# Audio tower in fp32: widened inverse sums, remainder tiles packed two at a time, and expert rows turned by VectorE

## The reference

```python
h = tok(x)                     # 16 sequences of 128 tokens, 256 features; conv of stride 2, mean, layer norm
h = h + attn0(layernorm(h))    # 16 heads of 16, causal window of 64, softmax, output projection
h = h + ffn0(layernorm(h))     # 16 experts, top 2, F = 352, 320 slots an expert, plus a shared FFN of F = 352
h = h + attn1(layernorm(h))    # 16 heads of 16, causal
h = h + ffn1(layernorm(h))     # 64 experts, top 3, H = 1024, 128 slots an expert, gelu, biases

# ffn0, per expert e: xs[320, 256] are the rows sent to e
y = (silu(xs @ w_gate[e]) * (xs @ w_up[e])) @ w_down[e]      # 352 = 128 + 128 + 96; 320 = 128 + 128 + 64
# attention, per head: out = (exp(scores) @ v) / sum(exp(scores))
```

## Time and profile before

| what | value |
|---|---|
| runs | 1119.18, 1120.36, 1120.80 us |
| median | 1120.36 us |
| span of the profiled execution | 1118.0 us |
| busy: PE, PEld, DVE, ACT, POOL | 1073.2, 906.5, 488.1, 525.8, 320.7 us |
| 0 to 38 us | first loads and the first pair, PE filling up |
| 38 to 200 us | first attention, convolution and router beside it |
| 200 to 230 us | shared FFN, last scatters |
| 230.46 to 422.58 us | the 16 experts of the first FFN |
| 422.58 to 606 us | shared FFN's rest and second attention |
| 606 to 642 us | its end, scatters, first rows of the 64 experts |
| 642.28 us to the end | the 64 experts |

### The profile page before, as it was taken

The page is one execution under the profiler, slowest core; times in us unless marked ns, Lnnn a source line. Parts: engine busy times, 40 slices in busy tenths (PEclk is TensorE's granted clock), DMA queues, the critical chain, the costliest instruction groups (busy, mean ns, idle before and its releaser), DMA issues.

```text
span 1118.0 us, 23799 instructions
## 1 busy us (share of the span) xinstructions
PE 1073.2 (96%) x7550; PEld 906.5 (81%) x7550; DVE 488.1 (44%) x2591; ACT 525.8 (47%) x1904; POOL 320.7 (29%) x317
## 2 busy tenths in 40 slices
PE   8999997999999999899998799999999999999996
PEld 7788876876666668677776699999999999999995
DVE  5779997622222323568988422222222222222221
ACT  2999999421112112999998033333323333332331
POOL 3222533413433442003226512222212222221222
PEclk9999999999999999999999899999999999999998
DMA  9932010156566644049101199999999998999980
GB/s 329 379 127 76 21 40 36 44 153 176 115 173 153 137 81 94 1 137 361 35 27 44 56 349 322 313 307 318 311 312 320 316 314 304 310 315 318 319 283 10
DMA packets 152006, 219.06 MB, mean 196 GB/s; under 512 B 15422, under 2 KB 124437, under 8 KB 151408
## 3 DMA queue, kind: packets, MB, share of 16 engines
q1 hardware_dynamic: 132976, 203.41, 53.2%
q0 software_dynamic: 18944, 14.62, 7.4%
HBM read 184.74 MB, written 43.09 MB: 204 GB/s over the span
## 4 chain that ended last, share of the span: by engine, by line
PE 79%; ACT 9%; DVE 3%; issue 3%; SPq 2%; DMA 2%; POOL 1%; POOLq 0%; DVEq 0%; ACTq 0%
PE bank L1075 21%; PE bank L1088 19%; PE bank L944 9%; PE bank L954 6%; ACT probs L1151 5%; PE bank L831 3%; PE bank L799 3%; PE bank L912 3%; PE bank L921 2%; PE bank L822 2%; PE bank L845 2%; PE bank L775 2%; PE bank L808 1%; PE bank L872 1%; PE bank L930 1%
## 5 line engine op out<-in xcount | busy, mean ns | idle before, releaser
L1318 ACT ACTIVATE dhidT<-bank,b1T 128x128 f32<-128x128 f32 x512 | 145.9, 368 | 308.9 <-PE bank L1075 308.9
L1075 PE MATMUL bank<-probsT,arena 128*128 128x128 f32 x2048 | 240.9, 277 | 0.1
L1075 PEld LDWEIGHTS bank<-probsT,arena 128*128 128x128 f32 x2048 | 235.5, 193 | 0.4 <-DVE probsT L1738 0.3
L1088 PE MATMUL bank<-arena,dhidT 128*128 128x256 f32 x1024 | 231.5, 380 | 0.0
L1088 PEld LDWEIGHTS bank<-arena,dhidT 128*128 128x128 f32 x1024 | 190.1, 191 | 22.9
L747 POOL DMA_INDIRECT out<-probsT,slot_token x64 | 98.6, 1540 | 375.5 <-DMA out<-probsT,slot_token 299.1
L1151 ACT ACTIVATE probs<-probs,neg_max 128x128 f32<-128x128 f32 x512 | 197.7, 393 | 1.6 <-DVE neg_max L1424 1.4
L1756 DVE TENSOR_TENSOR probsT<-bank,b_wide 128x256 f32<-128x256 f32 x64 | 27.2, 425 | 346.3 <-PE bank L1088 346.3
L1424 DVE CUSTOM_DVE_ANT_0 probs<-bank,mask 128x128 f32<-128x128 f32 x512 | 112.7, 284 | 11.6 <-PE bank L822 11.1
L718 POOL DMA_INDIRECT stream<-arena,slot_token x48 | 72.6, 1513 | 128.9 <-DVE arena L1618 94.7
L944 PE MATMUL bank<-rowsT,arena 128*128 128x320 f32 (+1 forms) x384 | 108.9, 436 | 0.2 <-DVE arena L1609 0.2
(11 more groups left out here) (162 smaller groups left out, 1368.7 us busy)
## 6 DMA issues: line engine op xcount, KB each, us to landing
arena<-L_ffn_w SPq DMA_DIRECT2D x128, 1024.0 KB, 7.3
rows<-zeros SPq DMA_DIRECT2D x13, 1024.0 KB, 12.1
drows<-rows SPq DMA_DIRECT2D x64, 132.0 KB, 7.5
arena<-L_ffn_w_gate SPq DMA_DIRECT2D x16, 352.0 KB, 4.4
arena<-L_ffn_w_up SPq DMA_DIRECT2D x16, 352.0 KB, 5.5
early<-rows SPq DMA_DIRECT2D x16, 264.0 KB, 3.5
early<-x SPq DMA_DIRECT2D x8, 512.0 KB, 6.8
arena<-L_ffn_w_down SPq DMA_DIRECT2D x16, 256.0 KB, 2.8
```

Source lines behind the costliest of these rows:

```text
L1075: mm = pe.matmul(bank[2 + 2 * (u % 2) + half][:, jj * P:(jj + 1) * P], w1_sb[u][:, c, j * P:(j + 1) * P], drowsT[:, u % 2, c, :], start=c ...
L1088: last_ = pe.matmul(bank[6 + u % 2][:, 0:D], dhidT[:, u % 2, j, :], w2_sb[u][:, j, :], start=j == 0, stop=j == J1 - 1)
L1318: last_ = act.activation(dhidT[:, u % 2, j, :], bank[2 + 2 * (u % 2) + half][:, jj * P:(jj + 1) * P], ACT.Gelu, bias=b1T[:, j, bass.ds(e, 1)])
```

## The change

1. Inverse sums: GpSimd copies each inverse 16 times side by side (`widen`, L695, 128 x 256, twice a pair), PE transposes the wide tile (four 128 x 128, L867) straight into a job's bank, ACT copies it once. `own_rows`, `exp_invT`, the 16-row copy, the matmul by 0/1 and one job a pair are gone. The wait for `inv_done` on PE becomes one for `wide_done`, which GpSimd sets.
2. In the first FFN `keep_ffn_inT` writes `all_inT` directly, and router and shared FFN read it there; `keep_for_shared` is gone.
3. Expert rows: four DMAs (L528, 32 partitions x 10 x 64 words, runs of 256 bytes) lay the rows so that one DVE 32 x 32 block transpose (L1583, 128 x 640) gives them turned. The features come out in another order, and the weights' rows are put in that order. The meta words come with two DMAs of their own (L530, L531; runs of 32 bytes), read by `slots`. The six transposes on PE, the two copies on ACT and two jobs an expert are gone.
4. Gate and up weights are one array and one DMA (L507, 720,896 bytes). Its columns are gate 128, up 128, gate 128, up 128, gate 64, up 64, gate 32, up 32. Block j = 2 is now one 128-row product (L945, 320 columns: gate 64 and up 64) and one of 64 rows whose two column halves (160 each) go to the two halves of the partitions (L948). In `down`, the block of 64 slots is done in two column halves of 128, one on each half of the partitions (L964).
5. silu of j = 2 covers 128 x 480, its product is three DVE instructions instead of one, the scaling of the last slot block two instead of one.
6. All five order tables are new, and so is the list of jobs (one INVERSE a pair, no SPREAD, no ROWS).

The diff without the tables and the renumbered lines:

```diff
         exp_inv = sb("exp_inv", [P, 2, HEADS])
-        own_rows = sb("own_rows", [P, D])
-        exp_invT = sb("exp_invT", [P, 2 * P])
+        exp_wide = sb("exp_wide", [P, 2, HEADS, HD])
         inv_rows = sb("inv_rows", [P, DC, 2 * P])
...
+        def turned_input(L, i):
+            return all_inT[:, :, 2 * P * i:2 * P * (i + 1)] if L is L0 else ffn_inT[:, :, :]
         def later(i, u):
...
                 s = ew_in[u]
-                sp.dma_start(gate_w[u], a["L0_ffn_w_gate"][bass.ds(e, 1)].rearrange("a (c p) f -> p (a c) f", c=DC)).then_inc(s, 16)
-                sp.dma_start(up_w[u], a["L0_ffn_w_up"][bass.ds(e, 1)].rearrange("a (c p) f -> p (a c) f", c=DC)).then_inc(s, 16)
+                sp.dma_start(gate_up_w[u], a["L0_ffn_w_gate_up"][bass.ds(e, 1)].rearrange("a (c p) f -> p (a c) f", c=DC)).then_inc(s, 16)
...
                 u = e % 3
-                wait_written(sp, EXPERTS, (e - 3, ROWS), (e - 3, ROWS + 1))
+                wait(sp, e_turned, e - 2)
+                own = rows0[bass.ds(e * C0, C0), 0:D].rearrange("(a j) d -> j a d", j=32)
+                for q in range(4):
+                    sp.dma_start(erows[32 * q:32 * (q + 1), u, :].rearrange("p (a d) -> p a d", a=RB), own[:, :, 64 * q:64 * (q + 1)]).then_inc(er_in[u], 16)
                 wait(sp, e_slots, e - 2)
-                sp.dma_start(erows[:, u, 0:full, :], rows0[bass.ds(e * C0, full * P)].rearrange("(s p) d -> p s d", p=P)).then_inc(er_in[u], 16)
-                sp.dma_start(erows[0:C0 - full * P, u, full, :], rows0[bass.ds(e * C0 + full * P, C0 - full * P)]).then_inc(er_in[u], 16)
+                sp.dma_start(emeta[:, u, 0:full, :], rows0[bass.ds(e * C0, full * P), D:ROW].rearrange("(s p) d -> p s d", p=P)).then_inc(em_in[u], 16)
+                sp.dma_start(emeta[0:C0 - full * P, u, full, :], rows0[bass.ds(e * C0 + full * P, C0 - full * P), D:ROW]).then_inc(em_in[u], 16)
...
+            def widen(L, i, t):
+                pool.wait_ge(L.inv_done, 2 * i + t + 1)
+                wait_written(pool, L, (i - 1, INVERSE))
+                g.tensor_copy(exp_wide[:, t, :, :], over(exp_inv[:, t, :], 2, [P, HEADS, HD])).then_inc(L.wide_done, 1)
             def scatter(L, i):
...
-                pe.wait_ge(L.inv_done, 2 * i + 2)
+                pe.wait_ge(L.wide_done, 2 * i + 2)
                 bk, full = new_job(L, i, INVERSE)
-                for t in range(2):
-                    last = pe.transpose(bk[0:HEADS, t * P:(t + 1) * P], exp_inv[:, t, :], ident[:, :])
-                last.then_inc(full, 1)
-            def spread_inverse(L, i):
-                bk, full = new_job(L, i, SPREAD, (i, INVERSE))
-                for m in range(DC):
-                    last = pe.matmul(bk[:, m * D:(m + 1) * D], own_rows[:, m * P:(m + 1) * P], exp_invT[:, :],
-                                     start=True, stop=True)
+                wide = exp_wide[:, :, :, :].rearrange("p t h d -> p t (h d)")
+                for c in range(DC):
+                    for t in range(2):
+                        last = pe.transpose(bk[:, (2 * c + t) * P:(2 * c + t + 1) * P], wide[:, t, c * P:(c + 1) * P], ident[:, :])
                 last.then_inc(full, 1)
...
                 f, m = FT[j]
-                pe.wait_ge(L0.input_kept, p + 1)
+                wait_read(pe, L0, (p, TURN_FFN))
                 bk, full = new_job(SHARED, p, GATE_UP + j)
...
-            def turn_rows(e, c):
-                pe.wait_ge(er_in[e % 3], 32 * (e // 3 + 1))
-                bk, full = new_job(EXPERTS, e, ROWS + c)
-                for s, (r, m) in enumerate(CT):
-                    last = pe.transpose(bk[:, r:r + m], erows[0:m, e % 3, s, c * P:(c + 1) * P], ident[0:m, 0:m])
-                last.then_inc(full, 1)
             def gate_up(e, j):
...
                 wait(pe, e_hid, n - 1)
-                for w, dst in ((gate_w[e % 2], score_bank[2 * (n % 2)]), (up_w[e % 2], score_bank[2 * (n % 2) + 1])):
+                w, dst = gate_up_w[e % 2], score_bank[2 * (n % 2):2 * (n % 2) + 2]
+                if j < 2:
+                    for half in range(2):
+                        f = (2 * j + half) * P
+                        for c in range(DC):
+                            last = pe.matmul(dst[half][:, 0:C0], w[:, c, f:f + P], rowsT[:, e % 2, c, :], start=c == 0, stop=c == DC - 1)
+                else:
+                    for c in range(DC):
+                        pe.matmul(dst[0][:, 0:C0], w[:, c, TAIL:LAST], rowsT[:, e % 2, c, :], start=c == 0, stop=c == DC - 1)
                     for c in range(DC):
-                        last = pe.matmul(dst[0:m, 0:C0], w[:, c, f:f + m], rowsT[:, e % 2, c, :], start=c == 0, stop=c == DC - 1)
+                        for part_ in range(2):
+                            last = pe.matmul(dst[0][64 * part_:64 * (part_ + 1), C0:C0 + CH], w[:, c, LAST:2 * F0],
+                                             rowsT[:, e % 2, c, CH * part_:CH * (part_ + 1)],
+                                             start=c == 0, stop=c == DC - 1, skip_group_check=True)
                 last.then_inc(e_gu, 1)
...
                 for j, (f, fm) in enumerate(FT):
-                    last = pe.matmul(bk[0:m, 0:D], hidT[e % 2][0:fm, j, r:r + m], down_w[e % 2][0:fm, j, :], start=j == 0, stop=j == NFT - 1)
+                    if s < 2:
+                        last = pe.matmul(bk[0:m, 0:D], hidT[e % 2][0:fm, j, r:r + m], down_w[e % 2][0:fm, j, :], start=j == 0, stop=j == NFT - 1)
+                    else:
+                        for c in range(DC):
+                            last = pe.matmul(bk[64 * c:64 * (c + 1), 0:P], hidT[e % 2][0:fm, j, r:r + m], down_w[e % 2][0:fm, j, c * P:(c + 1) * P],
+                                             start=j == 0, stop=j == NFT - 1, skip_group_check=True)
                 last.then_inc(full, 1)
...
-                bk, free = from_job(L, i, INVERSE, (i - 1, SPREAD))
-                act.activation(exp_invT[0:HEADS, :], bk[0:HEADS, 0:2 * P], ACT.Copy).then_inc(free, 1)
-            def keep_spread(L, i):
                 wait(act, L.mix_done, i)
-                bk, free = from_job(L, i, SPREAD)
+                bk, free = from_job(L, i, INVERSE)
                 act.activation(inv_rows[:, :, :], bk[:, :].rearrange("p (c n) -> p c n", c=DC), ACT.Copy).then_inc(free, 1)
...
-                if L is L0:
-                    wait(act, L0.input_kept, i)
-                bk, free = from_job(L, i, TURN_FFN, (i - 1, ROUTE))
-                act.activation(ffn_inT[:, :, :], bk[:, :].rearrange("p (c n) -> p c n", c=DC), ACT.Copy).then_inc(free, 1)
-            def keep_for_shared(i):
-                wait_read(act, L0, (i, TURN_FFN))
-                act.activation(all_inT[:, :, bass.ts(i, 2 * P)], ffn_inT[:, :, :], ACT.Copy).then_inc(L0.input_kept, 1)
+                bk, free = from_job(L, i, TURN_FFN, *(((i - 1, ROUTE),) if L is L1 else ()))
+                act.activation(turned_input(L, i), bk[:, :].rearrange("p (c n) -> p c n", c=DC), ACT.Copy).then_inc(free, 1)
...
-            def keep_rows(e, c):
-                wait(act, e_gu, NFT * (e - 1))
-                bk, free = from_job(EXPERTS, e, ROWS + c)
-                act.activation(rowsT[:, e % 2, c, :], bk[:, 0:C0], ACT.Copy).then_inc(free, 1)
             def silu_b(e, j):
...
                 n = NFT * e + j
                 act.wait_ge(e_gu, n + 1)
                 wait(act, e_hid, n - 1)
-                act.activation(silu[n % 2][0:m, :], score_bank[2 * (n % 2)][0:m, 0:C0], ACT.Silu).then_inc(e_silu, 1)
+                size = C0 if j < 2 else C0 + CH
+                act.activation(silu[n % 2][:, 0:size], score_bank[2 * (n % 2)][:, 0:size], ACT.Silu).then_inc(e_silu, 1)
...
+            def turn_rows(e):
+                dve.wait_ge(er_in[e % 3], 64 * (e // 3 + 1))
+                wait(dve, e_gu, NFT * (e - 1))
+                dve.transpose(rowsT[:, e % 2, :, :].rearrange("p c (a j) -> p a c j", j=32),
+                              erows[:, e % 3, :].rearrange("p (a c i) -> p a c i", a=RB, c=DC)).then_inc(e_turned, 1)
             def slots_b(e):
-                dve.wait_ge(er_in[e % 3], 32 * (e // 3 + 1))
-                slots(erows[:, e % 3, :, :], e % RING1, e, e, slot_steps, e_slots)
+                dve.wait_ge(em_in[e % 3], 32 * (e // 3 + 1))
+                slots(emeta[:, e % 3, :, :], e % RING1, e, e, slot_steps, e_slots, 0)
...
                 n = NFT * e + j
                 dve.wait_ge(e_silu, n + 1)
                 wait_written(dve, EXPERTS, (e - 2, DOWN + 2))
-                dve.tensor_tensor(hidT[e % 2][0:m, j, :], silu[n % 2][0:m, :], score_bank[2 * (n % 2) + 1][0:m, 0:C0], ALU.mult).then_inc(e_hid, 1)
+                hid, act_, (first, second) = hidT[e % 2], silu[n % 2], score_bank[2 * (n % 2):2 * (n % 2) + 2]
+                if j < 2:
+                    last = dve.tensor_tensor(hid[:, j, :], act_[:, 0:C0], second[:, 0:C0], ALU.mult)
+                else:
```

(22 more changed lines are left out.)

759 lines of the change are left out of this document (375 added, 384 removed).

## The result

The changed kernel takes 1090.37 us (median of four, 1089.38 to 1091.9), the kernel before 1119.93 beside it: ratio 0.9736, 95% interval 0.9725 to 0.9748, faster by 29.6 us. I had said 1081 (1068 to 1102). The direction and the range were right, 9 us of the 39 were missing.

> The changed kernel itself, as the level for the others of this call: 1089 to 1092 us.

The account below looks back on a forecast made before the run. PE alone was taken to bound the experts, PE then ACT the first attention, ACT the second. Savings of 30.3 + 5.1 + 2.9 + 0.6 = 38.9 us from the 1118.0 span, plus 2.4 to the median, gave 1081 (1068 to 1102).

Parts of the forecast that it names:

- the attention gains nothing: Rival, both attentions: POOL's late copies or waits set by the new orders lose 8.0 us, giving 1089.5; chance 0.06.
- the add chain: Rival, experts: POOL's adds, each waiting for the previous landing, set the period at up to 10.65 us: 1093.7; chance 0.13.
- PE's terms in the experts: Experts on PE: gate and up 6.26 us, down 3.44, so 9.70 an expert instead of 11.87; stage saves 35.2.
- The rule on draining: Experts on PE: a tiling-mode change drains TensorE; 0.2 us taken per added pair; no drain would be 3 us better.
- The start: First expert: PE waits for the first rows' transfer and DVE's turn before `gate_up(0, 0)`; 1.9 us lost.
- The feeds: Experts: weight loads queued behind row loads on SP sometimes land late for PE; 3 us lost in all (0 to 8).
- the weights' 9.7 against 9.70: Experts: SP's issues and landings up to the next weights take 9.7 us, the same as PE's period of 9.70.
- Second attention, -2.9: Second attention, taken as ACT bound: dropping eight 16 x 256 inverse copies of 0.356 us saves 2.9 us.
- First attention, -5.1: First attention, where PE is full: the new inverse transposes save 0.64 us a pair, 5.1 us in all.
- the sign that I gave: Expected in the changed kernel's profile: ACT still full in both attentions, each some 3 to 5 us shorter.
- Tail, -0.6: Tail: the 3.50 us gap ahead of a late scatter, waiting for DVE's slots, shrinks; 0.6 us of at most 2.7.
- the slower rival: Rival, experts: SP's short-run row loads take 1.6 us per issue and delay the weights, giving 1150; chance 0.04.

Follow-up runs that it names:

- the second profile: Profile from a second measurement of the changed kernel, nothing altered: 1090.48 us, ratio 0.9734 to the kernel before.
- e_warm2: Changed kernel plus 25 unread 128 x 128 products on PE during its wait before the second attention: 1087.74 us, against 1090.48 for the changed kernel beside it.
- e_keep_again: Changed kernel with ACT's second copy of the first FFN's turned input put back, on a slower chip: 1135.45 us, ratio 0.9699 to the kernel before.
- e_inv_copy: Changed kernel plus a 16 x 256 ACT copy ahead of each of eight widened-inverse copies in the second attention, slower chip: ratio 0.9731 to the kernel before.

## Why the prediction was right, and where it fell short

- **The number.** Inside the range, but the range is 34 us wide, and 1090.4 comes nearest to two rivals (1089.5, the attention gains nothing; 1093.7, the add chain) by neither's working. That it lies inside is in part luck.
- **PE's terms in the experts.** Right. Gate and up 6.30 us (I had 6.26), down 3.26 (3.44): the earlier trace rows carried it. With the waits the stage took 161.6 us, where I had said 157 to 160. The pair of shape changes that I took at 0.2 is at most 0.15 by L948's row (0.70 against 0.55 by length) and 0.01 by L964's.
- **The rule on draining.** The Trainium skill, TensorEngine Tiling (Array Packing), Key Properties, says that a change of mode drains TensorE. A drain may also lie in the records behind it: an expert takes 9.56 us, 0.26 more than its records by length (9.30), so all changes together cost here at most 4.2 us over 16 experts.
- **The start.** Right: `gate_up(0, 0)` waited 1.04 us for DVE's turn (1.43 in the second profile), where I had 1.9.
- **The feeds, 3.0 (0 to 8).** The size was low, 5.4, and the mechanism another: in the changed kernel mostly turned rows that DVE gives late. The prediction took DVE as covered because its busy time (6.3 of 9.7) fits; it was busy only 5.0 us an expert, and what PE waited for was the place of the turn in DVE's written order. With another order, 5.2 us of PE waits are left behind another releaser, which fits the weights' 9.7 against 9.70 of the prediction, though no trace names them. So two near ties probably lay on top of each other.
- **The add chain: the step that failed.** The prediction took it as a rival with a chance of 0.13, and priced it only as something that holds PE up in the experts (1093.7). It never asked who waits for its last link. Before, 3 of 16 experts' adds waited for a landing (the earlier trace rows shows two of them); at PE's 9.56 us an expert 13 did, which by the prediction's own signs is the add chain (it had expected L724 to be released by DVE more often). The chain fell 5.9 us further behind PE, and the second attention, which needs the whole stream, began 5.7 us later than forecast, 4.6 of it lost at the join. The sum had no term for the join. One add fewer is worth 10.6 us after and 1 before: that settles that the chain is the cause of the late start, and of those 10.6 some 2 lie in the experts, where the rival had looked.
- **The clock.** After the wait PE ran at the lower level for 4 to 5 us, and the first exponential came 1.3 us later still. No term for it either; the price is 1.5 to 3 us by the two profiles and `e_warm2`'s (its time, 2.7 less, agrees but doesn't show it alone).
- **Second attention, -2.9.** It shows as 1.1 us from first to last exponential (156.3 to 155.2). ACT is full there: busy 153.99 of 156.33 us before, 153.20 of 155.20 after. Only seven of the eight copies (2.5 us) stood in that stretch, and two other copies of ACT (`keep_v` and `keep_normedT`, 1.2) now stand behind the first exponential that stood ahead of it before, so 1.3 was to be had there. Whether the rest came back ahead of the first exponential can't be read beside the lower clock.
- **First attention, -5.1.** PE was free for the experts 4.8 us earlier (3.1 in the second profile), so the size is about right. But in 168 to 196 ACT isn't full any more (24.53 of 28.00) and PE does more (25.95), against the sign that I gave; `e_keep_again` agrees, on the other chip, that ACT's five microseconds weren't to be had in full.
- **Tail, -0.6.** From last exponential to the first L1082 it is 37.3 us, before 36.5. The gap of the earlier trace rows ahead of the last two inputs' scatters went, as I had said, but the last input's scatters then wait 3.92 us for DVE's slots, and those for the router. Not shown apart.
- **Last stage.** 474.0 instead of 475.7: its first 32 records take 3.84 us where the earlier trace rows has 5.46, so it begins at the full clock in this run. I had left it as it was. The change doesn't secure it: `e_warm2`, with the same work there, has 5.47 and 475.6.
- **Short runs.** The Trainium skill, DMA: Bandwidth & Descriptors, Specifications, says that transfers under 512 bytes don't reach line rate. The row loads land in 3.5 us at the median, as before, though each carries 80 KB and L525 carried 264; the slowest takes 7.8 (4.9 before). Longer runs gained nothing, so no cost in time shows here. L528's issue is 0.46 at the median and 1.62 at most, so the slower rival did not come.

## What to carry to other kernels

When a stage gets shorter, list every chain that runs beside it with its period, not only the engines' busy shares; a chain with 2 us to spare an iteration has none when the stage loses 2, and its backlog is paid where somebody waits for its last link. Count in the trace how many of its links already wait for each other. An order written for one set of durations hides such work by chance: after a change of durations, read the joins between stages again and fill the wait with work that is ready.

## What the hardware showed beyond that

- PE idled 6.15 us, and the granted clock went from 1.00 to 0.50; it came back between 412 and 414, some 4 us after PE had started again. With 25 products in the gap (`e_warm2`) it stayed at 1.00.
- Two 64-column tiles overlap even when all products of one stand ahead of the other's in the queue: L948 0.70 us for 8 records in both orders; `down`'s 12 short ones 0.66 in turn, 0.92 one half after the other, 1.30 by length one by one.
- GpSimd's broadcast copy of 128 x 256 took 0.398 us, less than a third of its 128 x 512 add of two inputs (1.275); DVE's 128 x 640 block transpose 0.84.
- On one chip the kernel before took 4.3% longer (1167.63 against 1119.63). The second attention of `e_inv_copy` ran there at a granted clock of 0.93 with ACT at 84%, where on the first chip the changed kernel's ran at 1.00 with ACT at 99%: a stage need not be bound by the same engine on both.
